# The first layer item's projections moved into the last cross-attention iterations, with the first iterations put in another order

## The reference

```python
x = x + xattn(layernorm(x), ctx)       # 8 heads of 64, softmax over 77 keys
x = x + ffn(layernorm(x))              # as written; ffn holds its own residuals

# each of the 2 layers inside ffn:
h = shift_token(x)                     # second half of the channels one token later
q, k, v = split(h @ wqkv)              # 3 x 512 columns
q, k = l2norm(q) * qs, l2norm(k) * ks
q, k = rotary_xpos(q, k)
o = local_attention(q, k, v)           # windows of 128 tokens, each sees itself and the one before
x = x + o @ wo
h = layernorm(shift_token(x)) * lg + lb
a, g = split(h @ w1 + b1)
x = x + (a * gelu(g)) @ w2 + b2
```

## Time and profile before

| | |
|---|---|
| median of 3 runs | 1441.26 us (1439.08 to 1441.63) |
| the profiled execution | 1443.41 us, span from first to last instruction 1441.4 us |
| mean granted TensorE clock | 0.993 of full speed |
| busy share of the span | PE 97%, DVE 76%, ACT 65%, POOL 53% |
| stage 1 | until 258.8 us, iterations of 13.2 us in the steady part |
| change of stage, iteration g = 16 to the scores of the first layer item | 239.2 to 289.6 us |

### The profile page before, as it was taken

The page is one execution under the profiler, slowest core; times in us unless marked ns, Lnnn a source line. Parts: engine busy times, 40 slices in busy tenths (PEclk is TensorE's granted clock), DMA queues, the critical chain, the costliest instruction groups (busy, mean ns, idle before and its releaser), DMA issues.

```text
span 1441.4 us, 32911 instructions
## 1 busy us (share of the span) xinstructions
PE 1401.7 (97%) x11652; PEld 1253.9 (87%) x11652; DVE 1090.0 (76%) x3067; ACT 936.4 (65%) x2662; POOL 761.5 (53%) x576
## 2 busy tenths in 40 slices
PE   6999999899999999999999999999999999999988
PEld 6999998777888888888888888888888888888878
DVE  5677766357878888888878878888788878888874
ACT  4787776156666666666666767666666666666662
POOL 1121211446666666666666667766666666666643
PEclk9999999999999999999999999999999999999999
DMA  6133112000101100010010201111111111111001
GB/s 213 40 103 104 57 60 103 31 12 20 30 29 34 32 30 28 28 28 28 28 28 29 69 29 37 38 36 36 37 36 36 35 35 35 35 42 36 29 29 31
DMA packets 50517, 63.43 MB, mean 44 GB/s; under 512 B 8402, under 2 KB 32104, under 8 KB 50408
## 3 DMA queue, kind: packets, MB, share of 16 engines
q1 hardware_dynamic: 50408, 61.99, 13.7%
HBM read 38.17 MB, written 16.78 MB: 38 GB/s over the span
## 4 chain that ended last, share of the span: by engine, by line
PE 63%; DVE 9%; issue 3%; POOL 2%; ACT 2%; DMA 1%; SPq 1%; DVEq 0%; ACTq 0%; POOLq 0%
PE pb L550 29%; PE pb L856 7%; PE pb L870 6%; PE pb L832 6%; PE pb L801 5%; PE pb L816 5%; PE pb L894 4%; DVE p_t L1533 2%; DVE p_t L1547 1%; DVE r_sin L1520 1%; DVE n_sq L1500 1%; DVE r_cos L1514 1%; DMA x<-x 1%; ACT p_t L1171 1%; SPq L505 1%
## 5 line engine op out<-in xcount | busy, mean ns | idle before, releaser
L1755 POOL TENSOR_TENSOR n_inv<-n_cl,half_neg 128x16 f32<-128x16 f32 x64 | 211.0, 3297 | 177.9 <-DVE n_cl L1505 174.5
L1171 ACT ACTIVATE p_t<-p_t,s_nm 128x128 f32<-128x128 f32 (+1 forms) x512 | 226.9, 447 | 18.1 <-DVE s_nm L1533 16.8
L550 PE MATMUL pb<-h_hi,w_hi 128*128 128x256 f32 x704 | 207.2, 294 | 0.8 <-DVE hg L1557 0.8
L550 PE MATMUL pb<-h_hi,w_lo 128*128 128x256 f32 x704 | 198.6, 282 | 0.0
L550 PE MATMUL pb<-h_lo,w_hi 128*128 128x256 f32 x704 | 198.6, 282 | 0.0
L1760 POOL TENSOR_TENSOR r_cos<-r_cos,r_sin 128x1024 f32<-128x1024 f32 x64 | 154.6, 2416 | 61.2 <-DVE r_sin L1520 61.2
L1162 ACT ACTIVATE pt_t<-pb 128x512 f32<-128x512 f32 x192 | 114.5, 597 | 99.9 <-PE pb L816 99.1
L1127 ACT ACTIVATE qk_sq<-pb 128x512 f32<-128x512 f32 x128 | 72.4, 591 | 158.5 <-PE pb L550 158.5
L1533 DVE CUSTOM_DVE_ANT_0 p_t<-pb,mask_t 128x128 f32<-128x128 f32 (+1 forms) x512 | 151.8, 352 | 25.7 <-PE pb L801 25.5
L1786 POOL TENSOR_TENSOR hg_lo<-hg,hg_hi 128x256 fp32r<-128x256 f32 (+1 forms) x192 | 142.4, 763 | 47.8 <-DVE hg_hi L1564 47.8
L550 PE MATMUL pb<-wqkv_hi,xt_hi 128*128 128x512 f32 x384 | 164.3, 428 | 1.9 <-DVE r_sin L1520 1.9
(11 more groups left out here) (145 smaller groups left out, 3936.4 us busy)
## 6 DMA issues: line engine op xcount, KB each, us to landing
y_state<-x SPq DMA_DIRECT2D x32, 256.0 KB, 2.1
x_cur<-y_state SPq DMA_DIRECT2D x32, 256.0 KB, 2.6
x_res<-y_state SPq DMA_DIRECT2D x32, 256.0 KB, 2.8
x_in<-x SPq DMA_DIRECT2D x16, 256.0 KB, 2.9
x_state<-x SPq DMA_DIRECT2D x16, 256.0 KB, 2.1
x_orig<-x_state SPq DMA_DIRECT2D x16, 256.0 KB, 2.9
out<-x SPq DMA_DIRECT2D x16, 256.0 KB, 2.2
x<-x SPq DMA_DIRECT2D x32, 112.0 KB, 2.3
```

The source lines that it names most:

```text
L550: mm = pe.matmul(dst, s, m, start=(n == 0 and k == 0), stop=(n == len(pairs) - 1 and k == 2))
L1171: e = nc.scalar.activation(pu, pu, ACT.Exp, bias=s_nm[:, j, k:k + 1], scale=-1.0, accum_out=s_sum[:, j, k:k + 1])
L1755: nc.gpsimd.tensor_tensor(n_inv[:, t], n_cl[:, t], half_neg[:], ALU.pow).then_inc(pool_inv, 1)
```

## The change

There are two parts.

**The start.** ScalarE and VectorE split `xq` before the turned rows of sequence 0; the statistics and the turning of sequence 1 come before the split and the product of the context's values. Splitting the second context group (`c_round(1)`, `c_rests(1)`) and `xo` goes from iteration 0 to iteration 1, behind work of the attention. The 21 constants are loaded in iteration 1 (`load_consts`), after `load_qkv(0)`, so the second context group and input 2 are issued earlier. GpSimd adds the first bias rows only once sequence 1 is normalised.

**The change of stage.** Item 0 of the layers is turned in g = 16 after `x_out(14)`, and its six projections are spread over g = 16 (k and q of the first token half, v, then q and k of the second half) and g = 17 (the last v). `FIRST_BANK` gives them banks 2 to 5, so that they stay clear of 6 and 7, where `x_values` sums. The item's squares, rotations, sums and GpSimd's `rotated` move with them; `y_normed(15)` moves to layer iteration 0. Of the idle products all of g = 16 and 17 and 5 + 18 of layer iteration 0 go, and of the 86 there remain 42. `x_cur` for item 1 is loaded in g = 16. `x_iterations(run_x)` is called further down on each engine, because `run_x` now uses helpers that are defined after it.

The core of the diff (the rest of it only takes `project`, `square`, `copy_v`, `rotate`, `squares` and `clamp` of item 0 out of the layer iteration with `not is_first(a)`):

```diff
+        FIRST_BANK = {(0, 0): 4, (0, 1): 5, (0, 2): 2, (1, 0): 2, (1, 1): 3, (1, 2): 4}
+        def is_first(n):
+            return isinstance(n, int) and n == 0
+        def qkv_bank(a, t, part):
+            return FIRST_BANK[t, part] if is_first(a) else part
+        def xt_bank(n):
+            return 4 if is_first(n) else 3
...
                 if g == 0:
                     load_c(1)
-                    sp.wait_ge(w_lo, WEIGHT["xv"])
-                    load_b(0)
                 if g in (GROUP, 2 * GROUP):
...
+                if g == SEQS:
+                    sp.wait_ge(pe_xt, 1)
+                    sp.dma_start(x_cur[:], one(y_dram, 1)).then_inc(cur_load, 16)
...
                 if g == 0:
+                    sp.wait_ge(w_lo, WEIGHT["xv"])
+                    load_b(0)
+                if g == 1:
                     sp.wait_ge(w_lo, WEIGHT["xo"])
                     load_qkv(0)
+                    load_consts()
...
-                if has_next(a):
+                if has_next(a) and not is_first(a):
                     sp.wait_ge(pe_xt, at(a, 1, 1))
                     sp.dma_start(x_cur[:], one(y_dram, seq_of(plus(a, 1), layer))).then_inc(cur_load, 16)
...
+                    x_turn(1)
                     x_values_of(0)
-                    x_turn(1)
                     return
                 if b is not None:
                     x_scores(b, was, 0)
                 if a is not None:
                     x_queries(a, 0)
                 if g == SEQS + 1:
-                    turn_x(0)
-                if g >= SEQS:
-                    idle_products(8, 4)
+                    project(0, None, 1, 2)
                 if d is not None:
                     x_out(a, d)
                 if g == 1:
+                    pe.wait_ge(x_cv, 1)
                     idle_products(12, 7)
+                if g == SEQS:
+                    turn_x(0)
                 if b is not None:
                     x_scores(b, was, 1)
                     x_probs(b, 0)
+                if g == SEQS:
+                    pe.wait_ge(xt_zero, 1)
+                    pe.wait_ge(w_lo, WEIGHT["w10c"])
+                    project(0, None, 0, 1)
...
                     if g == SEQS:
-                        idle_products(14, 4)
+                        project(0, None, 0, 0)
+                        pe.wait_ge(x_exp, at(b, XUNITS, XUNITS))
+                        project(0, None, 0, 2)
                     x_probs(b, 2)
+                    x_probs(b, 3)
                     if g == SEQS:
-                        idle_products(8, 4)
-                    x_probs(b, 3)
+                        project(0, None, 1, 0)
+                        project(0, None, 1, 1)
...
-                    if isinstance(a, int) and a == 0:
-                        pe.wait_ge(x_res1, SEQS)
-                    else:
+                    if not is_first(a):
                         pe.wait_ge(act_qkt, at(plus(a, -1), 4, 3 if part == 1 else 4))
+                elif is_first(a):
+                    if part == 0:
+                        pe.wait_ge(act_v, 1)
+                    elif part == 2:
+                        pe.wait_ge(dve_rope, 1)
...
-                elif k == 3 and c is None:
+                elif k == 1 and is_first(a):
+                    pe.wait_ge(act_v, NT)
+                elif k == 3 and c is None and not is_first(a):
                     pe.wait_ge(act_v, at(a, NT, NT))
...
-                if isinstance(g, int) and g < 2:
+                if isinstance(g, int) and g == 1:
                     idle_products(5, 7)
...
-                if isinstance(g, int) and g < 2:
-                    idle_products(18 if g == 0 else 6, 7)
-                if a is not None:
+                if isinstance(g, int) and g == 1:
+                    idle_products(6, 7)
+                if a is not None and not is_first(a):
...
+                if is_first(a):
+                    pe.wait_ge(dve_rope, NT)
                 if has_next(a):
                     turn_next(a, b, c)
-                if isinstance(g, int) and g == 0:
-                    idle_products(86, 7)
+                if is_first(a):
+                    idle_products(42, 7)
+                    pe.wait_ge(x_res1, SEQS)
...
                 if g == 0:
-                    x_turned(0)
                     act.wait_ge(xq_in, 16)
                     split_hi("xq", raw_a[:, 0:KC * INNER].rearrange("p (c n) -> p c n", c=KC), xq_hi[:])
+                    x_turned(0)
...
+                    x_turned(1)
                     x_values_copy(0, 0)
-                    x_turned(1)
-                    act.wait_ge(raw_a_in, 16)
-                    split_hi("xo", raw_a[:, KC * INNER:KC * INNER + IC * D].rearrange("p (c n) -> p c n", c=IC), xo_hi[:])
-                    c_round(1)
...
+                if g == 1:
+                    c_round(1)
+                    act.wait_ge(raw_a_in, 16)
+                    split_hi("xo", raw_a[:, KC * INNER:KC * INNER + IC * D].rearrange("p (c n) -> p c n", c=IC), xo_hi[:])
...
+                if g == SEQS:
+                    x_hi(0)
                 if b is not None:
                     x_exps(b, 2)
                     x_exps(b, 3)
+                if g == SEQS:
+                    square(0, 0, 1)
+                    square(0, 0, 0)
+                if b is not None:
                     x_probs_copy(b, 0)
                     x_probs_copy(b, 1)
...
+                if g == SEQS:
+                    copy_v(0, 0, 0)
                 if a is not None:
                     x_values_copy(a, par)
                 if next_keys(a):
@@ -1102,13 +1139,18 @@
                     x_queries_copy(a, par, 1)
                 if a is not None and a < SEQS - 1:
                     x_turned(a + 1)
+                if g == SEQS:
+                    square(0, 1, 0)
+                    square(0, 1, 1)
+                if g == SEQS + 1:
+                    copy_v(0, 1, 0)
                 if b is not None:
...
                     x_normed(0, 0)
+                    split_lo("xq", raw_a[:, 0:KC * INNER].rearrange("p (c n) -> p c n", c=KC), xq_hi[:], xq_lo[:])
                     x_turned_lo(0)
-                    split_lo("xq", raw_a[:, 0:KC * INNER].rearrange("p (c n) -> p c n", c=KC), xq_hi[:], xq_lo[:])
                     split_lo("xk", xk_raw, xk_hi[:], xk_lo[:])
                     c_rests(0)
-                    split_lo("xv", xv_raw, xv_hi[:], xv_lo[:])
                     x_stats(1, 1)
                     aggregate(x_mv[:, 0], x_st[:, 0], x_bst, x_bmv, 1)
+                    split_lo("xv", xv_raw, xv_hi[:], xv_lo[:])
                     x_normed(1, 1)
                     x_turned_lo(1)
-                    split_lo("xo", raw_a[:, KC * INNER:KC * INNER + IC * D].rearrange("p (c n) -> p c n", c=IC), xo_hi[:],
-                             xo_lo[:])
-                    c_rests(1)
                     return
                 if b is not None:
                     x_maxes(b, 0)
@@ -1425,14 +1462,19 @@
                     x_inverse_sums(b, 1)
                     x_norm_probs(b, 0)
                 if g == SEQS + 1:
-                    x_lo(0)
+                    squares(0, 1)
+                    clamp(0, 1)
                 if d is not None:
...
+                if g == SEQS:
+                    x_lo(0)
                 if b is not None:
                     x_maxes(b, 2)
                     x_norm_probs(b, 1)
                     x_maxes(b, 3)
+                if g == 1:
+                    c_rests(1)
...
+                if g == 1:
+                    split_lo("xo", raw_a[:, KC * INNER:KC * INNER + IC * D].rearrange("p (c n) -> p c n", c=IC), xo_hi[:],
+                             xo_lo[:])
...
+                if g == SEQS:
+                    dve.wait_ge(const_made, 2 * LAYERS)
+                    dve.wait_ge(x_bias, SEQS)
+                    rotate(0, 0, 0)
+                    squares(0, 0)
+                    clamp(0, 0)
+                if d is not None and d < SEQS - 1:
                     y_normed(d)
+                if g == SEQS:
+                    rotate(0, 1, 0)
                 if b is not None:
                     x_out_lo(b, 0)
                     x_out_lo(b, 1)
...
+                if is_first(a):
+                    y_normed(SEQS - 1)
...
                 if g == 0:
                     pool.wait_ge(bo_in, 16)
+                    pool.wait_ge(x_norm, 2)
                     x_bias_rows(0, 0)
                     x_bias_rows(1, 1)
+                if g == SEQS:
+                    pool.wait_ge(x_pv, SEQS)
+                    nc.gpsimd.memset(xt_hi[:, T:T + 1].bitcast(F32), 0.0)
+                    nc.gpsimd.memset(xt_lo[:, T:T + 1].bitcast(F32), 0.0).then_inc(xt_zero, 1)
+                if g == SEQS + 1:
+                    rotated(0, 1)
                 if d is not None:
                     deviation(x_mv[:, 1, :, 1], x_ve[:, 1], x_rs[:, 1], d, y_bmv, d + 1, y_eps, y_rst)
...
+                if g == SEQS:
```

(5 more changed lines are left out.)

123 lines of the change are left out of this document (55 added, 68 removed).

## The result

The changed kernel takes 1418.44 us (1417.01 to 1420.19, five runs), the kernel before 1441.63 in the same session: the ratio is 0.9847, 95% interval 0.9836 to 0.9858. The forecast was 1414.3 with a range of 1410 to 1421. The profiled execution took 1418.82 with a span of 1416.7, so 24.7 us are gone from the span, where 27.0 were forecast. On the medians it is 23.2: the profiled execution of the kernel before lay 2.15 us over its median, this one 0.4.

What follows compares the result with a forecast made beforehand. TensorE's work was taken to bound the steady part and layers, so earlier starts move all that follows: 9.0 us (start) plus 18.0 (change of stage) make 27.0, 1441.26 to 1414.3 us; range 1410 to 1421, own range 1411 to 1416.

Steps and rivals of the forecast that it cites:

- Power blocks: Rival at the change of stage: GpSimd's power holds up VectorE's `y_normed(14)`, losing 2.4 us: 1416.7; 0.20 shared with clock rival.
- Clock at the seam: Rival: TensorE's 1.4 us pause before `x_out(15)` lowers its clock, costing 2.8 us: 1417.1; chance 0.20 shared with power rival.
- slower: Rival: with fewer idle products TensorE's clock stays low from 259 through the first layer iterations, 33 us: 1447; chance 0.03.
- Not what it says: Rival: item 0 is early, but item 1's load or sequence 15's store holds layer iteration 1: 1429 to 1441; chance 0.03.
- the steady part at 198.7 us again: Sign for stage 1's steady attention iterations: their stretch keeps its length of 198.7 us.
- from there to the end of the span the same 1151.8: Sign for the layers: first layer scores to the span's end takes 1151.8 us as before.
- an iteration of 13 us of room: Start: the store and inputs queued behind SyncE's 21 constants have 13 us of slack, so were costed at nothing.
- start half won: Rival: the clock falls at the start too, or an input or weight is late: gain 4 to 6.1, 1417 to 1419; 0.12.
- wrong if that last stretch is longer: Refuting sign: first layer scores to the span's end exceeds 1151.8 us, through the clock or a late load.

Runs made afterwards that it cites:

- e7: Changed kernel with SyncE's list of the kernel before; the other engines' lists stay changed: 1426.24 us, ratio 0.9897 against the kernel before.
- e8: Changed kernel with TensorE, VectorE, ScalarE and GpSimd start lists as before, only SyncE's list changed: 1419.91 us, ratio 0.9857 against the kernel before.
- e6: e3 with item 0's two sums on VectorE, second half's squares and clamp before its rotation, 4 idle products instead of 42: 1413.79 us.
- e5: e3 without the 42 idle products TensorE runs while GpSimd finishes item 0: 1416.32 us, ratio 0.9836 against the kernel before.
- e3: Changed kernel with the input load two sequences on moved ahead of the normalised rows' store in SyncE's list: 1417.88 us, ratio 0.9841 against the kernel before.
- e11: Changed kernel with 42 instead of 12 idle products in attention iteration 1: 1420.90 us, ratio 0.9860 against the kernel before.
- e9: e6 with VectorE's `xo_lo_t` ahead of the second rotation and 9 idle products of 384 columns instead of 4 of 128: 1414.17 us.
- e10: e3 with 14 idle products of 384 columns in place of the 42 of 128 columns: 1421.99 us.
- e12: e9 with 22 idle products of 128 columns in place of the 9 of 384: 1412.04 us, ratio 0.9805 against the kernel before.

## Why the prediction was right, step by step

**The start** was forecast at 9.0 us and is 9.2. First scores 18.6 forecast, 18.01 measured; maxima 19.7, 19.16; second half 22.8, 22.29; scores of sequence 1 at 31.6, 31.37. But e7 and e8 show that my account of it was half a reason. I followed the wait for the context's rest and no other. The queue alone gives more than the lists alone, because the input of sequence 2 was late as well: VectorE waited for it at 29.65 in the kernel before, behind the wait that I followed. For the lists without the queue I still expected 7 to 8 us (e7), and they gave 1.2. So the 9.2 came out right although the second wait was never costed: the queue's new order, of which the prediction used only the context's earlier landing, took it away too. The clock's part is shown in e8: with a pause of 2.39 us it falls, with 0.22 it does not.

**The change of stage** was forecast at 32.4 us from iteration 16 to the first layer scores and is 32.28. Rotation after 11.8, measured 11.95; GpSimd's chain 14.6 to 15.5, measured 14.83; pause before `x_out(15)` 1.4, measured 1.43; idle products and GpSimd within a microsecond, measured 0.1.

**Power blocks** did not happen: `y_normed(14)` ran from 248.38 in 0.72 us, and GpSimd's power from 248.55 in 3.01. `n_cl` was held by the sum as forecast (1.33 us, and 2.07 for the second at 253.86); with the sums on VectorE (e6) it takes 0.18 both times. By the rule of the Trainium skill quoted in the prediction ("SBUF — State Buffer", "SBUF: two separate sides") the power should have held VectorE too; the trace speaks against it once more. The Trainium skill makes a condition there for VectorE's side, two SBUF inputs or one of its two-port modes. That does not save the rule here: an instruction of `y_normed`'s form was held by GpSimd's sum (2.66 us in e8, below), and in e6 VectorE's own sum of two SBUF tensors, in its list from 250.56, took its usual 1.21 us inside the power of 249.78 to 252.68.

**Clock at the seam** and **slower**: the pause of 1.43 us left the clock at 1.00. e5 has the pause that the slower rival needed, 4.65 us, and it cost 1.9 us, not 33: the clock was back by the first layer scores. **Not what it says** did not happen either: layer iteration 1 takes 31.71 us before and after.

**What failed** is "the steady part at 198.7 us again" and "from there to the end of the span the same 1151.8". The first lost 1.5 us, and e3 and e11 show why: TensorE's list was changed, so its instruction blocks are fetched at other moments, and three of them met the issue of an input that VectorE needs at once. I had costed the later inputs at nothing with "an iteration of 13 us of room"; the load is issued about 3 us before it is wanted, and even behind an issue of 0.39 us VectorE waited for it in some iterations (0.44 us at 65.06). There was no room. The kernel before already paid for this once: behind its long issue at 141.56 VectorE waited 0.98 us for the input, and that iteration took 14.75. The layers gave 1.1 back. They are the same code in all these kernels and take 1150.2 to 1155.3 us; two profiles of one kernel agree (1152.9, 1152.7). Part of it is the clock at the end, up to 2.2 us. The other part is in single iterations, and they go with the same packets. In the fourteen profiles, 76 of the 434 layer iterations 1 to 31 take over 0.15 us longer than the shortest of the same number. In 67 of them a DMA issue in the first 6 us meets a q8 packet and ends 0.25 to 0.45 us after it; of the other 358, 4 have one. The changed kernel has 5.0 us of such excess (iterations 4, 7, 16, 19 and 23), the kernel before 2.3 (5, 14, 17, 20 and 23): the 2.7 us.

Iteration 7 shows the way. It takes 36.67 us in the changed kernel, with a packet from 476.36 to 477.32, and 35.29 in e5, with no packet near. The last, smallest piece of the rows shifted by one token (0.5 KB) takes 3.1 us from issue to landing in the one and 1.7 in the other. VectorE's statistics wait for it; the changed kernel, then e5:

```profile
478.39 0.75 DVE L1529 BATCH_NORM_STATS2 l_st<-x 128x6 f32<-128x256 f32 x2 [2.99 <-DMA x<-x]
```

```profile
476.14 0.75 DVE L1529 BATCH_NORM_STATS2 l_st<-x 128x6 f32<-128x256 f32 x2 [1.62 <-DMA x<-x]
```

TensorE then stops for 0.46 us at 481.95, waiting for VectorE. The other iterations are a count and not an experiment, and nine long ones have no such issue.

These two terms are 2.6 us; the start and the seam gave 0.3 more than forecast, so the span lost 2.3 us less. The rest of the miss on the median (1418.44 against 1414.3) is 1.8 us: the forecast took 2.15 us off for the profiled execution's place over the median, and the measured one lay 0.4 over it. So 1418.4 is outside the forecast's own 1411 to 1416 and inside the full range only by its margin for errors. It falls where "start half won" was priced (1417 to 1419), and that did not happen; the number's place there is chance. By its own sign, "wrong if that last stretch is longer", the prediction failed in the layers by 1.1 us.

A slip that changed no term: I divided the steady part by 15 iterations of 13.24 us; it is 14 of 14.19, and so 14.2 us an iteration, not 13.2, in the table of the profile before.

## What to carry to other kernels

A DMA issue that several instructions wait for soon after should stand as early in its queue as its buffer allows. Here one moved load took out every wait for inputs, and the six kernels that have it (e3, e5, e6, e9, e10, e12) keep a steady part of 197.5 to 197.7 us. In four of them a packet met the context load of iteration 8, whose issue took 1.35 to 1.89 us, and that iteration stayed under 14.2. Their lists up to the seam are the same, so other places of the code were not tried. When a wait is removed, look for the next wait behind it on the same engine: two late inputs can hide behind one row, and then each fix alone is worth little. When a part of the kernel that nobody edited changes its length by 1 to 5 us in 1400, look for the packets and the clock before giving it to the edit. When idle products fill a wait on another engine, shorten that engine's chain first, then cut the filler to what is left.
